# The second half of each attention layer norm moves from VectorE to GpSimd

## What is computed

```python
x = x + L0_ffn(L0_cond(x, cond_64, ...))          # 8 experts, 2 per token, 2 shared; ternary weights
x = x + L1_ffn(L1_cond(x, bias, mask, ...), ...)  # attention; quantised gated FFN

def L1_cond(x, attn_bias, mask, g_in, null_attn_bias, null_kv, Wq, Wkv, Wo, g_out):
    xn = layernorm(x, g_in)          # (x - mean) * rsqrt(var + 1e-5) * g, per token
    q  = xn @ Wq                     # 16 heads of 64, one shared key/value head
    k, v = split(xn @ Wkv)           # one null key and value in front of them
    sim = q k^T / 8 + bias           # causal and padding mask
    out = softmax(sim) v @ Wo
    return layernorm(out, g_out)
```

## Time and profile before

| | before |
|---|---|
| median of 3 runs | 1423.92 us (1421.58 to 1424.39) |
| the profiled execution's own time | 1425.79 us |
| its span, first to last instruction | 1423.9 us |
| mean granted TensorE clock | 0.958 |
| busy over the span | PE 88%, DVE 73%, ACT 54%, POOL 39% |

### The profile page before, as it was taken

How to read it: one execution, slowest core, us unless ns; L and a number is a source line. 1 busy time by engine, 2 the same in 40 slices (tenths; PEclk the granted TensorE clock), 3 DMA queues, 4 the chain that set the end, 5 groups by cost and what they waited for, 6 DMA issues and landing times. The chain is left out here.

```text
span 1423.9 us, 29590 instructions
## 1 busy us (share of the span) xinstructions
PE 1253.1 (88%) x8705; PEld 995.0 (70%) x8710; DVE 1036.8 (73%) x2790; ACT 771.5 (54%) x1949; POOL 557.3 (39%) x838
## 2 busy tenths in 40 slices
PE   4899999999884899999999999999999999934866
PEld 2778888888773777887877787777788788821223
DVE  5666666667645877888877878867878878664986
ACT  3333333333232666776766676766676776625853
POOL 1543333333232874454453454443543544500014
PEclk9999999999997899999999999999999999977986
DMA  6323112320204500010010000010010000102215
GB/s 233 104 93 104 69 36 103 119 75 16 89 1 148 171 2 2 2 32 1 1 32 2 2 31 2 1 33 1 2 31 2 16 2 20 58 15 64 59 60 177
DMA packets 51048, 71.61 MB, mean 50 GB/s; under 512 B 4498, under 2 KB 43667, under 8 KB 48852
## 3 DMA queue, kind: packets, MB, share of 16 engines
q1 hardware_dynamic: 50340, 69.60, 14.7%
q10 hardware_dynamic: 560, 0.20, 0.1%
HBM read 57.07 MB, written 12.72 MB: 49 GB/s over the span
## 5 line engine op out<-in xcount | busy, mean ns | idle before, releaser
L1082 POOL TENSOR_SCALAR scores<-scores,att_rinv 128x128 f32<-128x128 f32 (+3 forms) x512 | 265.8, 536 | 190.6 <-DVE att_rinv L1295 190.6
L1144 ACT ACTIVATE scores<-scores,att_top 128x128 f32<-128x128 f32 (+3 forms) x512 | 281.5, 553 | 85.4 <-DVE att_top L1277 85.1
L1277 DVE CUSTOM_DVE_ANT_0 scores<-ps_y,w_bias_b,w_null_s 128x128 f32<-128x128 f32 x448 | 229.3, 547 | 80.3 <-PE ps_y L1425 73.5
L301 POOL TENSOR_TENSOR act_w<-act_g,wide_w 128x512 f32<-128x512 f32 x64 | 105.8, 1653 | 282.0 <-DVE act_g L454 267.5
L1152 ACT ACTIVATE keep<-ps_up 128x128 f32<-128x128 f32 (+3 forms) x256 | 112.0, 438 | 170.7 <-PE ps_up L1436 167.4
L1436 PE MATMUL ps_up<-ident,scores 128*128 128x128 f32 x1280 | 190.8, 275 | 7.8 <-DVE keep L1305 7.0
L214 ACT ACTIVATE hid_hi<-hid 128x512 fp32r<-128x512 f32 x80 | 50.5, 632 | 245.5 <-DVE hid L472 245.5
L1436 PEld LDWEIGHTS ps_up<-ident,scores 128*128 128x128 f32 x1280 | 151.4, 141 | 28.5 <-issue 13.7
L1447 PE MATMUL ps_a<-keep,w_val 128*64 128x128 f32 x2560 | 170.1, 280 | 0.7 <-DVE keep L1305 0.7
L1447 PEld LDWEIGHTS ps_a<-keep,w_val 128*64 128x64 f32 x2560 | 138.9, 138 | 21.6 <-issue 18.6
L1513 PE MATMUL ps_gate<-w_wo,o_t 128*128 128x256 f32 x512 | 139.6, 392 | 0.0
(11 more groups left out here) (315 smaller groups left out, 2942.8 us busy)
## 6 DMA issues: line engine op xcount, KB each, us to landing
wide_w<-token_w_dram SPq DMA_DIRECT2D x16, 1024.0 KB, 4.6
x_raw<-in_x_t_dram SPq DMA_DIRECT2D x8, 512.0 KB, 3.7
x_nat<-in_x_nat_dram SPq DMA_DIRECT2D x8, 512.0 KB, 4.6
x_dram<-x_nat SPq DMA_DIRECT2D x8, 512.0 KB, 2.9
w_x1t<-x_dram SPq DMA_DIRECT2D x8, 512.0 KB, 4.3
c_dram<-out_raw SPq DMA_DIRECT2D x8, 512.0 KB, 3.2
c2t<-c_dram SPq DMA_DIRECT2D x8, 512.0 KB, 3.6
x_tile<-x_dram SPq DMA_DIRECT2D x8, 512.0 KB, 4.4
```

Of the source, the lines that this page charges most:

```text
L301: nc.gpsimd.tensor_tensor(act_w[:, k % 2], act_g[:, k % 2], wide_w[:, k], ALU.mult).then_inc(sem.act_w_ready, 1)
L1082: nc.gpsimd.tensor_scalar(s, s, rinv[:, pp, q, hh:hh + 1], 0.0, ALU.mult, ALU.add).then_inc(sem.p_normed, 1)
L1144: nc.scalar.activation(s, s, ACT.Exp, scale=-1.0, bias=top[:, pp, q, hh:hh + 1], accum_out=lsum[:, pp, q, hh:hh + 1]).then_inc(sem.exp_don ...
L1277: dve.tensor_tensor_reduce(scores_of(pp, hh, q), psS[:, hh, 0:n], bias_of(w, h)[:, CAUSAL[q]:CAUSAL[q] + n], 1.0, null_s[:, par, q, h:h + ...
```

## The change

DVE keeps the statistics and the aggregation. `moments` has three stages: two tiles, two tiles, aggregation. From the variance on POOL does the work: `reciprocal_deviation` in three stages, with four instructions for an iteration (six in the first stage, with epsilon and seed) instead of three, and `standardise` in two halves. Two new semaphores, in_moments and out_moments, go from DVE to POOL; ln_ready and out_normed are now signalled by POOL. The tables of steps are new.

```diff
+def moments(dve, x, stat, mean_var, stage):
+    if stage < 2:
+        for t in range(2 * stage, 2 * stage + 2):
+            last = dve.bn_stats(stat[:, t], x[:, t])
+    else:
+        dve.drain()
+        for t in range(TT):
+            last = dve.bn_aggr(mean_var[:, t], stat[:, t])
+    return last
+
+def reciprocal_deviation(pool, mean_var, work, seed, stage):
+    var, y, a = work[:, 0], work[:, 1], work[:, 2]
+    if stage == 0:
+        pool.tensor_scalar(var, mean_var[:, :, 1], EPS, 0.0, ALU.add, ALU.add)
+        pool.drain()
+        pool.tensor_scalar(seed[:], var.bitcast(I32), -0.5, RSQRT_SEED, ALU.mult, ALU.add)
+    now = seed[:].bitcast(F32) if stage == 0 else y
+    pool.drain()
+    pool.tensor_tensor(a, now, now, ALU.mult)
+    pool.drain()
+    pool.tensor_tensor(a, a, var, ALU.mult)
+    pool.drain()
+    pool.tensor_scalar(a, a, -0.5, 1.5, ALU.mult, ALU.add)
+    pool.drain()
+    pool.tensor_tensor(y, a, now, ALU.mult)
+
+def standardise(pool, x, mean_var, work, half):
+    pool.drain()
+    for t in range(2 * half, 2 * half + 2):
+        last = pool.tensor_scalar(x[:, t], x[:, t], mean_var[:, t, 0:1], work[:, 1, t:t + 1], ALU.subtract, ALU.mult)
+    return last
...
-        NORM_IN = (2, 2, 3, 3, 4, 4, 5, 6)
-        NORM_OUT = (13, 14, 15, 16, 17, 18, 19, 20)
+        NORM_IN, ROOT_IN, IN_SCALED = (1, 2, 2), (2, 3, 4), (4, 5)
+        NORM_OUT, ROOT_OUT, OUT_SCALED = (13, 14, 14), (15, 16, 17), (18, 19)
...
+                def root_in(f, stage):
+                    if stage == 0:
+                        pool.wait_ge(sem.in_moments, f)
+                        settle(pool)
+                    reciprocal_deviation(nc.gpsimd, mean_var, work, seed, stage)
+
+                def standardise_in(half):
+                    last = standardise(nc.gpsimd, x1t, mean_var, work, half)
+                    if half:
+                        last.then_inc(sem.ln_ready, 1)
...
                     if i % 4 == 2 and (ahead or i < STEPS - 4):
                         query_copy(PAIRS * b + i // 4 + 1, (i // 4 + 1) % 2)
+                    for stage in range(3):
+                        if ahead and i == ROOT_IN[stage]:
+                            root_in(b + 1, stage)
+                        if behind and i == ROOT_OUT[stage]:
+                            root_out(b - 1, stage)
                     for half in range(2):
+                        if ahead and i == IN_SCALED[half]:
+                            standardise_in(half)
+                        if behind and i == OUT_SCALED[half]:
+                            standardise_out(half)
                         if behind and i == SCALE_OUT[half]:
                             scale_out(b - 1, half)
...
                     normalise(J, j)
+                for stage in range(3):
+                    root_out(B - 1, stage)
+                standardise_out(0)
+                standardise_out(1)
                 scale_out(B - 1, 0)
                 scale_out(B - 1, 1)
...
-                    last = layer_norm(nc.vector, x1t, stat, mean_var, work, seed, stages)
-                    if LN_STAGES - 1 in stages:
-                        last.then_inc(sem.ln_ready, 1)
+                    last = moments(nc.vector, x1t, stat, mean_var, stage)
+                    if stage == 2:
+                        last.then_inc(sem.in_moments, 1)
```

More of the change, by code:

```diff
@@ L1090, in query_copy, with root_out, standardise_out @@
                                                 ALU.mult, ALU.add).then_inc(sem.qm_ready, 1)
+                def root_in(f, stage):
[3 more added lines that the diff above has]
+                    reciprocal_deviation(nc.gpsimd, mean_var, work, seed, stage)
+                def root_out(b, stage):
+                    if stage == 0:
+                        pool.wait_ge(sem.out_moments, b + 1)
+                        settle(pool)
+                    reciprocal_deviation(nc.gpsimd, mean_var, work, seed, stage)
+                def standardise_in(half):
+                    last = standardise(nc.gpsimd, x1t, mean_var, work, half)
+                    if half:
+                        last.then_inc(sem.ln_ready, 1)
+                def standardise_out(half):
+                    last = standardise(nc.gpsimd, out_raw, mean_var, work, half)
+                    if half:
+                        last.then_inc(sem.out_normed, 1)
                 def scale_out(b, half):
@@ L1316, in query_lo, with norm_in @@
                                                 f32(q_hl[pp][0:D, hh]), ALU.subtract).then_inc(sem.ql_ready, 1)
-                def norm_in(f, stages=range(LN_STAGES)):
-                    if 0 in stages:
+                def norm_in(f, stage):
+                    if stage == 0:
                         dve.wait_ge(sem.x1_in, 16 * (f + 1))
-                    last = layer_norm(nc.vector, x1t, stat, mean_var, work, seed, stages)
-                    if LN_STAGES - 1 in stages:
-                        last.then_inc(sem.ln_ready, 1)
+                    last = moments(nc.vector, x1t, stat, mean_var, stage)
+                    if stage == 2:
+                        last.then_inc(sem.in_moments, 1)
                 def normed_lo(f, par, c):
@@ L1345, in keys_lo, with norm_out @@
                     nc.vector.nop(nofuse=True).then_inc(sem.kl_ready, 1)
-                def norm_out(b, stages=range(LN_STAGES)):
-                    if 0 in stages:
+                def norm_out(b, stage):
+                    if stage == 0:
                         dve.wait_ge(sem.out_ready, 2 * b + 2)
-                    last = layer_norm(nc.vector, out_raw, stat, mean_var, work, seed, stages)
-                    if LN_STAGES - 1 in stages:
-                        last.then_inc(sem.out_normed, 1)
+                    last = moments(nc.vector, out_raw, stat, mean_var, stage)
+                    if stage == 2:
+                        last.then_inc(sem.out_moments, 1)
                 def largest(b, half):
@@ L1373, in step @@
                         null_weights_lo(b - 1)
-                    if behind and i in NORM_OUT:
-                        norm_out(b - 1, [s for s, at in enumerate(NORM_OUT) if at == i])
+                    for stage in range(3):
+                        if behind and i == NORM_OUT[stage]:
+                            norm_out(b - 1, stage)
                     for half in range(2):
@@ L1379, in step @@
                     if ahead:
-                        if i in NORM_IN:
-                            norm_in(b + 1, [s for s, at in enumerate(NORM_IN) if at == i])
+                        for stage in range(3):
+                            if i == NORM_IN[stage]:
+                                norm_in(b + 1, stage)
                         for c in range(HC):
@@ L1404, in _ @@
                 quantise_ffn_weights(dve, nc, w, sem)
-                norm_out(B - 1)
+                for stage in range(3):
+                    norm_out(B - 1, stage)
                 largest(B - 1, 0)
@@ L2115, in named_semaphores @@
     sem.ln_ready = new("ln_ready")
+    sem.in_moments = new("in_moments")
+    sem.out_moments = new("out_moments")
     sem.xnt_done = new("xnt_done")
```

## The result

The changed kernel takes 1434.23 us (median of 5 runs, 1432.04 to 1436.82) against 1423.92 before: 1.0074 times as long, 95% interval 1.0059 to 1.0088. It is slower by 10.3 us, where 17.5 us less were forecast. The profiled execution took 1432.98 us, with a span of 1430.8. Lines shift: scores are now L1500 and L1501, `turn` L1512, `biased_max` L1350, `normalise` L1120, `query_copy` L1127, `scale_out` L1155; the root on POOL stands at L849 to L860, `standardise` at L867.

What follows compares the result with a forecast made beforehand. The prediction took DVE's order, not the PE, as the bound in steps 4 to 8. DVE's relief of -26.7 us plus POOL's costs 5.5, 1.3 and 2.4 gave -17.5: 1406.4 us, range 1397 to 1418.

Steps and rivals of the forecast that it cites:

- c: Price of one small dependent instruction of the root on POOL: 0.33 us, bounds 0.27 to 0.42.
- POOL decides: Rival: c above 0.49 makes the kernel slower, at the root between steps 2 and 6; 1437 at 0.6; chance 0.10.
- the forecast's own formula: All gains and costs summed as a function of c: -54.4 + 112c, giving -17.5 us.
- batch 0: POOL, nearly full with masks, is 2.3 us late at step 6; about 1.0 comes back from DVE; cost 1.3.
- the end: Behind the last batch nothing covers POOL's output norm: 6.9 us against DVE's 4.5, so 2.4 more.
- the output norm: Steps 18 to 20: DVE's relief gives 0.8 us a batch, 4.8 for six; POOL's work there costs nothing.
- DVE's order was the bound: Steps 4 to 8: the input norm on DVE delays the PE; moving it gives 3.3 us a batch, 19.8 for six.
- POOL's lateness: Input norm up to step 6's transposes: POOL is 0.9 us late a batch, 0.6 of it at step 4; cost 5.5.
- The spacing: Time between starts of POOL's small instructions in the root: 0.33 us; 0.45 or more would prove the forecast wrong.
- three signs of being wrong: Spacing 0.45 or more; batch 0 growing over 3 us; PE's steps 4 to 8 near 14 without waiting for POOL.
- Only recorded idle returns: Rival: only the PE's recorded idle time, 14.6 us, comes back, less 9.2 of costs: 1418.5; chance 0.07.
- The collisions turn round: Rival: busier POOL delays three small DVE instructions of `totals`, up to 1.8 us a batch: 1417; chance 0.07.

Runs made afterwards that it cites:

- e5_fast: The change, but POOL negates the mean once and adds it instead of subtracting; 1408.12 us, ratio 0.9877 to the kernel before.
- e6_fast_late: `e5_fast` with the input norm's root on POOL at steps 3, 4, 4 instead of 2, 3, 4; 1405.69 us, ratio 0.9856 to the kernel before.
- e10_best: `e6_fast_late` with the last batch's output norm and batch 0's input norm on DVE; 1401.86 us, ratio 0.9829 to the kernel before.
- e7_fast_tail: `e5_fast` with the last batch's output norm wholly on DVE; 1404.96 us, ratio 0.9860 to the kernel before.
- e11_slow_late: The change, subtraction kept, with the input norm's root on POOL at steps 3, 4, 4; 1435.91 us, ratio 1.0090 to the kernel before.

## Why the prediction was wrong

**The step that failed.** "A `standardise` instruction has two pointers: 0.18 + 0.22 + 2 x 0.09 = 0.57." It measured 1.22 us. The sum took the rate of 0.85 ns an element from multiplications and additions and carried it over to a subtraction, which no row had shown on POOL. The price had no bounds: only c had, and c was right. The mechanism of the loss was in the text, as the first rival ("POOL decides", on the right side, 0.10), but tied to the small instructions, whose 0.35 us alone would have left the kernel faster (-54.4 + 112 x 0.35 = -15.2). What decided was the other price in the same sum, and the chance of 0.10 covered c alone.

**How far it explains the miss.** With 1.22 and c = 0.35 in the forecast's own formula: two of the four instructions stand ahead of step 6, 1.3 in six batches, 7.8; batch 0 and the end 2.6 each; c 112 x 0.02 = 2.2. The sum goes from -17.5 to -2.3, which is not yet a loss. The terms of the profile stand at +8.7 (without the rest). Of the 11 between, 6.6 are the output norm, where I had written "nothing" for POOL: behind a `standardise` of 2.4 us the transposes of step 21 wait, 0.39 us in batch 5, and steps 20 and 21 together are 1.1 longer than without the subtraction. 2.0 are in the input norm (1.2 of them one batch with the clock at 0.89), 1.7 in batch 7, 0.6 in batch 0 and the end. That second omission has the same root: in `e5_fast`, with 0.55 us, the output norm gives the forecast 4.8.

**Right.** DVE's order was the bound in steps 4 to 8, and its relief is real. Steps 4 to 11, at a clock of 1.00 in all six batches of both profiles, took 27.05 us before and 23.95 in `e6_fast_late`, 3.1 less with POOL's lateness still in it; the forecast had 3.3 less 0.9. Steps 8 to 11 gave 0.6 of it, which I had not counted. The spacing: 0.33 forecast, 0.35 measured. The waits for POOL at steps 4 and 6 appeared where named, 0.57 and 1.60 us. The reads of step 4's scores did not get the DVE wait that I named; it came at steps 6 and 7 (0.37 and 2.46 us in batch 5). Step 20 took 2.58 against 2.4. Of the three signs of being wrong one came, batch 0 (+4.5 us, limit 3); the spacing did not reach 0.45, and steps 4 to 8 stayed at 14.7 with a wait for POOL.

**Too small also without the subtraction.** POOL's lateness: forecast 0.9 a batch. In `e5_fast` steps 4 to 11 exceed by 1.9 what batch 7's 10.69 and the turn's 0.60 with 11.68 for the rest would give (24.84 against 22.97). Step 4 carries 1.2 of it, which I put at 0.6; it is POOL's wait at step 2, and `e6_fast_late` removes it (3.60 against 2.43). Batch 0: forecast 1.3, 3.1 in `e5_fast`. Its steps 4 to 7 are 2.7 longer, and `e10_best` shows that these are the norm's. Its steps 8 to 11 ran at a granted clock of 0.75 there and 1.00 before, 1.2 us more. `e7_fast_tail` has the same instructions in batch 0 and the same 15.6 us in steps 4 to 7, but its steps 8 to 15 take 23.3 us against 26.6, and its batch 0 as a whole is as long as before the change. So only the 2.7 is firm. The end: forecast 2.4, measured 3.1, for 15 instructions instead of 14 and the hand-over.

**The other rivals.** "Only recorded idle returns" is refuted by `e6_fast_late`: a batch gave 3.1 in steps 4 to 11 and 0.8 in steps 20 to 23, more than its 2.0 + 0.3 of idle time. "The collisions turn round": DVE's small instructions of `null_shift` and `totals` together took 6.0 us a batch before, 7.3 in the change and 5.9 in `e5_fast`, so POOL's new work as such does not lengthen them.

**Luck.** With the form that the sum had assumed, the forecast -17.5 meets -16.8, but its terms do not all meet. In steps 4 to 11 DVE's relief was worth 4.1 us a batch (27.05 - 22.97) and not 3.3, and POOL's lateness cost 1.9 and not 0.9; the two misses cancel. The terms of the table add up to -13.6 in `e5_fast`, and the other 3.0 are in stretches where the kernels are alike.

## What to carry to other kernels

Price an instruction by a row that has the same operation, not only the same engine, size and operands; where no row has it, the term needs two bounds of its own and a rival that fails by it. Where a sum has several unknown prices, say for each at what value the sign turns: here the standardising instruction at 1.22 instead of 0.55 was worth 27 us (`e5_fast` against the change), all the doubt about c 17. And when moved work makes an engine late, try the cheapest equal form of the work before its place: the form was worth 27 us, the place 0.9 us a batch. Before a place is called worthless, compare batches of the same granted clock: `e11_slow_late` as a whole was not faster, its two batches at full clock were.
